# Batch 0's last latent attention moved into the last cross attention of batch 1, its norm in three ticks

## The chip, the cores and the metric

One core of a Trainium2 chip runs the whole program. The metric is the device time of one execution in microseconds, as the median of several; the profile is one execution more, with its own time. All data is float32, so each matmul shows as two instructions in the trace, while a transpose is one.

## The reference

The input x has 2 batches of 512 tokens of 128 values, the context has 2 batches of 77 keys of 64 values. The stages are a latent attention (L0), a cross attention (L1), a decoder of six layers (L2) and a last latent attention (L3). The change touches the last one:

```python
q = emb @ Wq + bq                     # emb: the decoder's output, per batch 512 x 128
k, v = latent @ Wk + bk, latent @ Wv + bv      # latent: the context, 77 x 64
w = softmax((q @ k.T) / sqrt(E), axis=tokens)  # over the 512 tokens, for each of the 77 keys
x = w @ v + emb
out = (x - mean(x)) * rsqrt(var(x) + 1e-6) * gamma + beta
```

Each decoder layer has self attention (16 heads), cross attention over the 77 keys (16 heads) and a feed-forward of 512 hidden units, each behind a layer norm and with a residual.

## The kernel before, in words

The decoder is one flat program for each engine. A planner (class Unit) counts ticks; at each tick it lists what is issued, and every engine walks through the ticks in the same order, skipping what isn't its own. Work is done in chunks of 128 tokens: a score matmul (line 1039), the masked minimum on VectorE (L1495), the exponentials on ScalarE (L1281), the scaling by the reciprocal of the sums on GpSimd (L673), the transposes ("turns", L1051), their evacuation into PT by VectorE (L1513 in the cross attention), and, for a group of four chunks, the "attend" matmuls which add into one PSUM bank, sum (L1081). A tick of the cross attention of batch 1 has a turn every second tick and an attend step in the others. TensorE's order within a tick is: scores, attend steps, early jobs, the turn, jobs. VectorE's order is: reciprocals, the evacuation of the turn of the tick before, jobs of the tick before (of "out", three ticks before), the scaling of the last values, norm steps, masked minima. ScalarE runs the jobs of the tick before, then the last exponential, then the chunk's exponentials, then the eviction of sum (L1313).

Around the change, in the last layer: x1 is tick 488, at which the cross attention of batch 1 starts; it ends at tick 512 ("after"). Batch 0's feed-forward is in it: hidden products (job h, L876) at 496 and 497, the output product (job out, L907) at 498, its add into X (L1409) by VectorE at tick 501. From 513 to 514 the last attend steps are issued. Then follows batch 1's chain: eviction of sum (514), transposes back (job fin, L859, tick 515), the add into X (L1409, tick 516), its norm (statistics L1333, L1337, L1339; the root on GpSimd, L634; scaling L1344; ticks 516 and 517), the turned norm (job xn, L871, tick 519; the copy L1165), the hidden products (521) with their evacuation (L1179), the output product (522) and the add.

The last latent attention of a batch has six steps, whose ticks the tuple LAST_AT gives, counted from x1 + 14 = 502 for batch 0 and from 526 for batch 1: transposes of X (job x3, L703, copied by ScalarE, L1176); the score product for all tokens (job s3, L896) with the minimum on VectorE (L1359); the exponential on ScalarE (L1123); the reciprocal of its sum and the scaling of the values on VectorE (L1365, L1367); the value product (job p3, L729) with its add into X (L1409); the norm z with gamma and beta behind it (function finish, L1522, L1525), after which the output transfer of the batch is issued (L616). Before the change batch 0 has these at ticks 514, 516, 516, 519, 520 and 521. PSUM results of the jobs rotate over three banks (W0 to W2). GpSimd also adds a bias to X after batch 1's norm (L686).

Of the kernel before, what the change touches and what calls it, by code (L numbers as in the profile page):

```python
# [143 lines left out]
AFTER_X0 = (0, 2, 3, 4, 5, 7)  # L144
AFTER_X1 = (2, 3, 4, 4, 5, 7)
LAST_AT = (12, 14, 14, 17, 18, 19)
FEED0 = ((8, 8, 9, 9), 10, (13, 14, 15, 17))
FEED1 = ((9, 9, 9, 9), 10, (18, 18, 20, 21))


class Unit:
# [90 lines left out]
            self.jobs[at + kv] += [("k", j, b, i), ("v", j, b, i)]  # L242
            self.jobs[at + keys] += [("G", j, b, i, 0), ("G", j, b, i, 1)]

    def last_attention(self, b, at, steps):

        turned, scores, exps, scaled, values, norm = steps
        self.jobs[at + turned].append(("x3", self.layers, b))
        self.jobs[at + scores].append(("s3", self.layers, b))
        self.late[at + exps].append(("exp3", b))  # L250
        self.late[at + scaled].append(("scale3", b))
        self.jobs[at + values].append(("p3", self.layers, b))
        assert values < norm
        self.normalise(at + norm, ("z", self.layers, b, 3), (0, 0, 0))

    def last_operands(self, at):
        for i, what in enumerate(("k3", "v3", "g3")):
# [7 lines left out]
    def place(self):  # L265
        for b in range(B):
            self.early[1 + 4 * b].append(("xn", 0, b, 0))
        first = [[(kind, 0, i) for kind in ("ck", "cv")] for i in range(3)] + [[("cG", 0, i, r) for r in range(2)] for i in range(3)]
        for events, dt in zip(first, WEIGHTS0_AT, strict=True):
            self.jobs[1 + dt] += events  # L270
        self.self_operands(0, 0, 1, (0, 2, 4, 6))
        for j in range(self.layers):
            s0, s1, x0, x1 = (self.start[j, k] for k in range(4))
            after = self.end[j, 3]
            for i, dt in enumerate(CV_AT if j > 0 else CV0_AT):
                self.jobs[s0 + dt].append(("cV", j, i // 3, i % 3))
            self.self_operands(j, 1, s0, SELF1_AT)
            self.after_attention(j, 0, 0, s1, AFTER_S0)
            self.after_attention(j, 1, 0, x0, AFTER_S1)
            if j + 1 < self.layers:  # L280
                for (kind, *i), dt in zip(WEIGHTS, WEIGHTS_AT, strict=True):
                    self.jobs[s1 + dt].append((kind, j + 1, *i))
                self.self_operands(j + 1, 0, x1, SELF0_AT)
            self.after_attention(j, 0, 1, x1, AFTER_X0)
            self.feed_forward(j, 0, x1, *FEED0)
            self.after_attention(j, 1, 1, after, AFTER_X1)
            self.feed_forward(j, 1, after, *FEED1)
            if j + 1 == self.layers:
                self.last_operands((s1 + 30, s1 + 31, s1 + 33))
                self.last_attention(0, x1 + FEED0[1] + 4, LAST_AT)  # L290
                self.last_attention(1, after + FEED1[1] + 4, LAST_AT)

    def place_wide(self):
# [1287 lines left out]
```

How the kernel before makes its waits and increments, by code:

```python
        @block.sync  # L470
# [89 lines left out]
            sp.dma_start(norm_b[:], col(a["L2_xattn_norm_b"])).then_inc(sem("norm_in"), 16)  # L560
            load_o(0)
            sp.dma_start(cross_bias[:].bitcast(I32), a["mask_Bx1xS2_if1"].rearrange("b a m -> a b m").broadcast_to([P, B, M]))\
              .then_inc(sem("cross_mask_in"), 16)
            sp.dma_start(b2[:], a["L2_xattn_ff_b2"][0:L].rearrange("(a l) p -> a l p", a=1).broadcast_to([P, L, E]))\
              .then_inc(sem("b2_in"), 16)
            def emptied(unit, event, l):
                sp.wait_ge(sem(unit.ring.free(event)), unit.ring.value(event, l))
            sp.wait_ge(sem("L1_done"), 1)
            load_cross_o(0)
            load_ff(0)
            sp.wait_ge(sem("X_biased"), B)
            load("L3", "Wk", "Wq", "bk", "bq", "Wv")
            load_rows("L3", bv["L3"], "bv")
            load_rows("L3", gam["L3"], "gamma")
            load_rows("L3", bet["L3"], "beta")
            sp.wait_ge(sem("flag"), 1)
            general = sp.value_load(flag[0:1, 0:1], min_val=0, max_val=1)
            with sp.If(general < 1):
                for j in range(L):
# [6 lines left out]
                                emptied(FAST, event, 0)  # L588
                            else:
                                sp.wait_ge(sem(PRE.free(event)), PRE.value(event, 0))
                        load_q(j + 1)
# [114 lines left out]
            def key_operands(s, bank, l=0):  # L706
                pe.wait_ge(*loaded(s, "Wk"))
                if s == "L3":
                    pe.wait_ge(*loaded(s, "Wq"))
```

## Time and profile before

| | us |
|---|---|
| median of 3 runs | 1084.78 |
| lowest, highest | 1083.2, 1084.96 |
| profiled execution | 1083.69 |
| its span, first to last instruction | 1081.9 |
| TensorE busy | 1025.6 (95%) |
| ScalarE busy | 804.2 (74%) |
| VectorE busy | 719.9 (67%) |
| GpSimd busy | 392.1 (36%) |

The span begins at the first instruction; all positions below are microseconds from there. The decoder ends with batch 1's last steps, so the last 35 us of the span are the place of interest. [...]

### The profile page before, as it was taken

The numbers are of one execution on the slowest core, as the hardware profiler recorded it, in microseconds if no ns is written. First come the engines' busy times: TensorE is split into PE (matmuls) and PEld (weight loads), VectorE is DVE, ScalarE is ACT, GpSimd is POOL, SyncE is SP. The second block draws the span as 40 slices with busy tenths as digits, with TensorE's granted clock in tenths as the row PEclk, the third lists the DMA queues.
The fourth block names the chain that finished last, engine by engine and source line by source line (L and its number), as shares of the span: only waits on it lengthen the run. The fifth ranks groups of instructions, "written<-read, shape, count | busy, mean of one in ns | idle before, by whom it ended". The sixth has DMA issues, their size and how long they took to land.

```text
span 1081.9 us, 20513 instructions
## 1 busy us (share of the span) xinstructions
PE 1025.6 (95%) x5146; PEld 605.4 (56%) x5146; DVE 719.9 (67%) x4492; ACT 804.2 (74%) x3518; POOL 392.1 (36%) x404
## 2 busy tenths in 40 slices
PE   7899999999999999999999999999999999999984
PEld 5555455665555655555655555655555556555553
DVE  4666778556778566677765678656678855678744
ACT  3586988666998576898676798666798866699831
POOL 4133443233443233443333344223344322344420
PEclk9899999999999999999999999999999999999997
DMA  8402000003100002200002200001300000000000
GB/s 231 139 6 66 1 21 1 1 1 86 59 21 1 1 1 79 67 1 21 1 1 79 67 1 21 2 1 56 90 1 21 1 2 1 21 1 2 1 1 23
DMA packets 31802, 32.39 MB, mean 30 GB/s; under 512 B 3982, under 2 KB 27710, under 8 KB 30910
## 3 DMA queue, kind: packets, MB, share of 16 engines
q1 hardware_dynamic: 28542, 28.38, 9.4%
q10 hardware_dynamic: 3136, 2.62, 0.8%
q8 instruction: 46, 0.75, 0.3%
q14 instruction: 78, 0.64, 0.2%
HBM read 30.47 MB, written 0.52 MB: 29 GB/s over the span
## 4 chain that ended last, share of the span: by engine, by line
PE 85%; DVE 6%; ACT 5%; issue 3%; POOL 1%; DMA 0%; DVEq 0%; SPq 0%; ACTq 0%
PE S L1039 23%; PE T L1051 11%; PE sum L1081 10%; PE W L852 8%; PE sum L1065 7%; PE W L876 4%; PE W L907 4%; PE W L794 3%; PE W L831 2%; PE W L814 2%; PE W L809 2%; PE W L871 2%; DVE Pb L1495 2%; DVE XN L1344 2%; ACT Pb L1281 2%
## 5 line engine op out<-in xcount | busy, mean ns | idle before, releaser
L1281 ACT ACTIVATE Pb<-Pb,mn 128x128 f32<-128x128 f32 (+1 forms) x1536 | 561.0, 371 | 39.1 <-DVE mn L1495 38.6
L673 POOL TENSOR_TENSOR Pb<-Pb,rsum 128x512 f32<-128x512 f32 (+2 forms) x336 | 324.8, 971 | 606.2 <-DVE rsum L1503 606.1
L1281 ACT ACTIVATION_READ_ACCUMULATOR Pb<-Pb,mn 128x1 f32 x1536 | 295.0, 192 | 0.0
L1495 DVE CUSTOM_DVE_ANT_0 Pb<-S,late_bias 128x128 f32<-128x128 f32 x768 | 175.9, 286 | 124.3 <-PE S L1039 124.0
L1051 PEld LDWEIGHTS T<-ident,Pb 128*128 128x128 f32 (+2 forms) x1296 | 164.0, 146 | 155.4 <-issue 124.1
L1039 PE MATMUL S<-GV,XT 128*128 128x512 f32 x384 | 199.1, 605 | 1.9 <-DVE mn L1495 0.8
L1051 PE MATMUL T<-ident,Pb 128*128 128x128 f32 (+2 forms) x1296 | 197.1, 273 | 1.4 <-POOL Pb L673 1.4
L1513 DVE COPY PT<-T 128x512 f32<-128x512 f32 (+1 forms) x240 | 155.9, 650 | 59.8 <-PE T L1051 59.6
L1495 DVE CUSTOM_DVE_ANT_0 Pb<-S,cross_bias 128x77 f32<-128x77 f32 x768 | 131.8, 232 | 64.8 <-PE S L1039 62.6
L1081 PE MATMUL sum<-PT,Vc 128*128 128x512 f32 (+2 forms) x264 | 135.1, 601 | 0.2 <-DVE PT L1513 0.2
L1039 PE MATMUL S<-Gc,XT 128*128 128x462 f32 (+1 forms) x288 | 125.7, 521 | 3.5 <-DVE mn L1495 2.1
L1495 DVE DVE_READ_ACCUMULATOR2_ANT mn<- 128x1 f32 x1536 | 126.3, 82 | 0.0
L1039 PEld LDWEIGHTS S<-GV,XT 128*128 128x128 f32 x384 | 61.8, 190 | 56.2 <-issue 41.2
L852 PE MATMUL W<-PT,GV 128*64 128x512 f32 x384 | 93.0, 605 | 0.0
L1065 PE MATMUL sum<-o_pair,saow 128*128 128x512 f32 x192 | 90.3, 592 | 0.0
L1292 ACT ACTIVATE PT<-T 128x512 f32<-128x512 f32 x96 | 56.4, 587 | 27.1 <-PE T L1051 26.3
L1039 PEld LDWEIGHTS S<-Gc,XT 128*128 128x128 f32 x288 | 45.6, 190 | 34.7 <-issue 22.2
L634 POOL TENSOR_TENSOR rstd<-veps,minus_half 128x4 f32<-128x4 f32 x40 | 40.5, 1012 | 67.0 <-DVE veps L1339 66.0
L1081 PEld LDWEIGHTS sum<-PT,Vc 128*128 128x128 f32 (+2 forms) x264 | 44.9, 190 | 27.8 <-issue 24.4
L1503 DVE RECIPROCAL rsum<-sums 128x4 f32<-128x4 f32 (+1 forms) x336 | 58.4, 174 | 0.9 <-ACT Pb L1281 0.6
L1065 PEld LDWEIGHTS sum<-o_pair,saow 128*128 128x128 f32 x192 | 35.6, 190 | 39.2 <-issue 39.2
L1179 ACT ACTIVATE hT<-W,small 128x512 f32<-128x512 f32 x48 | 32.9, 687 | 22.5 <-PE W L876 22.2
(173 smaller groups left out, 1067.7 us busy)
## 6 DMA issues: line engine op xcount, KB each, us to landing
sakv<-in_L_xattn_sa_kv SPq DMA_DIRECT2D x6, 1024.0 KB, 5.6
caq<-in_L_xattn_ca_q SPq DMA_DIRECT2D x6, 512.0 KB, 7.1
saq<-in_L_xattn_sa_q SPq DMA_DIRECT2D x6, 512.0 KB, 5.7
cakv<-in_L_xattn_ca_kv SPq DMA_DIRECT2D x12, 256.0 KB, 7.9
saow<-in_L_xattn_sa_ow SPq DMA_DIRECT2D x6, 512.0 KB, 4.3
w<-in_L_xattn_ff_w SPq DMA_DIRECT2D x12, 256.0 KB, 3.0
caow<-in_L_xattn_ca_ow SPq DMA_DIRECT2D x30, 96.0 KB, 2.7
GV<-in_mask_BxSxS_ik ACTq DMA_DIRECT2D x1, 1536.0 KB, 11.7
```

The source lines that it names most:

```text
L673: nc.gpsimd.tensor_tensor(rows, rows, r, ALU.mult).then_inc(sem(f"{unit.name}_weights"), 1)
L852: last = nc.tensor.matmul(w[half(h), :], v_own[:, b, p // TB, c:c + D], PT[:, g % 2, p % 2 * 2 + h, :], start=True, stop=True)
L876: last = nc.tensor.matmul(w[:], w1[:, f * P:(f + 1) * P], XT[:, b * T:(b + 1) * T], start=True, stop=True)
L1039: nc.tensor.matmul(S_ps[n % 2][:, 0:group.columns], XT[:, (b * TB + qt) * P:(b * TB + qt + 1) * P], keys, start=True, stop=True).then_inc( ...
L1051: last = nc.tensor.transpose(T_ps[n % 2][0:k1 - k0, t * P:(t + 1) * P], Pb[:, n % SLOTS, k0:k1], ident[:])
L1065: mm = nc.tensor.matmul(sum_ps[:], saow[:, p, :], o_pair[:, p % 2, :], start=(p == 0), stop=(p == NPAIR - 1))
L1081: mm = nc.tensor.matmul(sum_ps[:], vals, PT[0:k, g % 2, blk, :], start=(group.first and blk == 0), stop=(group.last and at_end))
L1281: last = nc.scalar.activation(Pb[:, s, t * w:(t + 1) * w], Pb[:, s, t * w:(t + 1) * w], ACT.Exp, bias=mn[:, s, t:t + 1], scale=-1.0, accum ...
L1292: nc.scalar.activation(PT[:, gr % 2, 0:group.blocks, qt * P:(qt + 1) * P], tiles(T_ps[n % 2][:, 0:group.blocks * P]), ACT.Copy)\
L1495: last = nc.vector.tensor_tensor_reduce(out=Pb[:, s, cols], in0=S_ps[n % 2][:, cols], in1=row_bias, scale=1.0, scalar=3.4e38, op0=ALU.add, ...
L1503: nc.vector.reciprocal(rsum[:, n % SLOTS, 0:k], sums[:, n % SLOTS, 0:k])\
L1513: nc.vector.tensor_copy(PT[:, gr % 2, 0:group.blocks, qt * P:(qt + 1) * P], tiles(T_ps[n % 2][:, 0:group.blocks * P]))\
```

## The change

The steps of batch 0's last latent attention get their own tuple, and the three steps of its norm are put on ticks of their own. Counted from tick 502, they are now at 502 (transposes), 504 (scores), 506 (exponential), 508 (scaled values), 509 (value product), and 511, 512 and 513 (norm: statistics; mean, variance and root; scaling and finish). Batch 1's stay as they are. No instruction is added or removed.

```diff
 LAST_AT = (12, 14, 14, 17, 18, 19)
+LAST0_AT = (0, 2, 4, 6, 7, 9)
...
-    def last_attention(self, b, at, steps):
+    def last_attention(self, b, at, steps, by_step=(0, 0, 0)):
...
         assert values < norm
-        self.normalise(at + norm, ("z", self.layers, b, 3), (0, 0, 0))
+        self.normalise(at + norm, ("z", self.layers, b, 3), by_step)
...
                 self.last_operands((s1 + 30, s1 + 31, s1 + 33))
-                self.last_attention(0, x1 + FEED0[1] + 4, LAST_AT)
+                self.last_attention(0, x1 + FEED0[1] + 4, LAST0_AT, (0, 1, 2))
                 self.last_attention(1, after + FEED1[1] + 4, LAST_AT)
```

## Rows read from the trace of the kernel before

**Rows 1.** The page: busy time of TensorE, and its share in 40 slices.
```profile
PE 1025.6 (95%) x5146; PEld 605.4 (56%) x5146; DVE 719.9 (67%) x4492; ACT 804.2 (74%) x3518; POOL 392.1 (36%) x404
...
PE   7899999999999999999999999999999999999984
```

**Rows 2.** The chain of waits from 1037 us: start, duration, piece.
```profile
1037.48 0.44 PE T L1051 x4
...
1039.11 1.05 PE sum L1081 x2
...
1040.49 0.86 PE sum L1081 x2
...
1042.87 3.57 PE sum L1081 x8
...
1046.46 0.70 ACT oT L1313
...
1047.29 0.64 PE W L859 x4
...
1050.29 0.69 DVE OP L1359
...
1054.14 2.05 PE W L729 x8
1056.19 5.34 PE W L876 x8
```

**Rows 3.** Timeline, 1047 to 1063 us: start, duration, engine, line, idle before.
```profile
1047.96 0.69 DVE L1409 TENSOR_TENSOR X<-W,X 128x512 f32<-128x512 f32 x1 [4.50 <-PE W L859]
...
1050.39 1.02 POOL L634 TENSOR_TENSOR rstd<-veps,minus_half 128x4 f32<-128x4 f32 x1 [8.44 <-DVE veps L1339]
...
1052.64 1.27 POOL L686 TENSOR_TENSOR X<-X,b 128x512 f32<-128x512 f32 x1 [1.23 <-DVE XN L1344]
...
1052.71 1.28 DVE L1367 TENSOR_SCALAR L0vo<-L0vo,orec 77x128 f32<-77x128 f32 x1
...
1053.55 0.78 ACT L1165 ACTIVATE XT<-W,small 128x512 f32<-128x512 f32 x1 [1.72 <-PE W L871]
...
1057.01 0.87 DVE L1333 BATCH_NORM_STATS2 stats<-X 128x6 f32<-128x128 f32 x4
...
1062.06 0.69 DVE L1525 TENSOR_TENSOR X<-X,L0bet 128x512 f32<-128x512 f32 x1
```

**Rows 4.** Timeline of batch 1's last latent attention, 1067 to 1079 us.
```profile
1067.60 0.60 ACT L1176 ACTIVATE XT<-W 128x512 f32<-128x512 f32 x1 [5.37 <-PE W L703]
...
1070.16 0.72 ACT L1123 ACTIVATE OP<-OP,omin 77x512 f32<-77x512 f32 x1 [1.97 <-DVE omin L1359]
...
1071.25 0.28 DVE L1367 TENSOR_SCALAR L0vo<-L0vo,orec 77x128 f32<-77x128 f32 x1
...
1071.68 1.13 PE L729 MATMUL W<-L0vo,OP 77*128 77x128 f32 x8 [2.28 <-DVE L0vo L1367]
...
1073.62 0.87 DVE L1333 BATCH_NORM_STATS2 stats<-X 128x6 f32<-128x128 f32 x4
...
1078.29 0.69 DVE L1525 TENSOR_TENSOR X<-X,L0bet 128x512 f32<-128x512 f32 x1
```

**Rows 5.** Timeline of the last cross attention, 1036 to 1044 us.
```profile
1036.94 0.68 DVE L1409 TENSOR_TENSOR X<-W,X 128x512 f32<-128x512 f32 x1
...
1041.25 0.70 POOL L673 TENSOR_TENSOR Pb<-Pb,rsum 128x308 f32<-128x308 f32 x1 [0.68 <-DVE rsum L1503]
...
1042.90 0.56 DVE L1513 COPY PT<-T 128x384 f32<-128x384 f32 x1 [0.63 <-PE T L1051]
```

**Rows 6.** Windows of TensorE: stretch, its length, PE busy, granted clock, DMA.
```profile
35.95:42.70 6.75, 6.75 (x27) 0.50 0.56 148
1048.90:1052.70 3.80, 0.00 (x0) 1.00 0.00 0
1053.10:1059.80 6.70, 6.07 (x16) 0.50 0.00 1
1060.00:1066.00 6.00, 5.22 (x36) 1.00 0.15 44
```

## The prediction

> **What bounds the kernel now.** I read the page first: TensorE is busy 95% of the span, and in the slices only the last, where PE shows 4, is loose [rows 1]. So work moved earlier goes from a loose stretch into a full one. The chain of waits shows where the border lies. Up to 1046.46 us every long piece is PE, one matmul group behind the other without a gap: this is the last cross attention of batch 1 [rows 2]. From 1046.46 on it passes from engine to engine, one small step each: eviction of the sum, four transposes, the add into X, the norm, again transposes, then batch 1's feed-forward, then batch 1's latent attention [rows 2, 3, 4]. Nothing else has to be done in that tail but batch 0's latent attention, which the change moves. In the tail the reader should look for two things: what of batch 0's work stands on the chain, and what it stands beside.
>
> Of its four parts one is on the chain. The value product of batch 0 (line 729, eight instructions, 2.05 us) runs from 1054.14 to 1056.19, and batch 1's first hidden product, which is behind it in TensorE's order, starts at 1056.19 [rows 2]. What that product needed was ready before: the copy of the turned norm into XT ran 0.78 us from 1053.55, so it ended at 1054.33, and 0.14 us later (the gap between the end of the eviction at 1047.16 and PE's next piece at 1047.29) the hidden product could have begun, at 1054.47 [rows 2, 3]. So 1056.19 - 1054.47 = 1.7 us hang on the moved work. The transposes, the score product and the minimum of batch 0 lie in waits of batch 1's chain: the minimum (0.69 us at 1050.29) ends at 1050.98, while GpSimd's root, on which the norm waits, takes 1.02 us from 1050.39 and ends at 1051.41 [rows 2, 3]. Batch 0's own last norm and its scaling (1057.01 to 1062.75) lie beside batch 1's feed-forward and free nothing when they go [rows 3].
>
> **Part one: what TensorE gets in the full stretch.** Three jobs go in. Transposes of X: four instructions, 0.44 us at the pace of the turns there [rows 2]. The score product with 512 columns: two instructions, 0.86 us, as each attend step of the same width [rows 2]. The value product: eight instructions of 128 columns; alone at full clock 1.13 us [rows 4], at the pace of the turns (0.11 each) 0.88 us [rows 2]. I take 0.95, as PE has other work on both sides of it. Sum 2.25 us. Their cost is the full sum, since PE has no gap there, except where a gap is behind them anyway.
>
> Does the cross attention stall besides? I followed the ticks. The transposes come when four more turns are to follow, at 1037.9, and need the add of batch 0's feed-forward, which ran from 1036.94 to 1037.62 [rows 5]: no wait. ScalarE's copy (0.60 us [rows 4]) is done near 1039.05, the score product starts near 1039.5: no wait. VectorE's minimum (0.69) then ends near 1041.1, and behind it is queued the reciprocal of the last chunk but one, on which GpSimd's scaling (0.70) and then a turn wait. Before, that stood clear; now the scaled chunk is there at about 1042.0, and PE comes to that turn at 1042.45, being 1.3 us later itself: slack 0.4 us. The exponential has nothing behind it on ScalarE but the eviction; from its start at 1070.16 to the end of the scaling at 1071.53 the second batch took 1.4 us [rows 4], so this can be done by 1042.9, VectorE's evacuation and reciprocal between them included. But the scaling's one instruction took 1.28 instead of 0.28 us in the first batch, where GpSimd's 1.27 us add ran beside it from 1052.64 [rows 3, 4]. Now GpSimd's last chunk (0.70 us [rows 5]) is beside it: it ends at 1043.2 at the worst, and PE reaches the value product at 1043.64. The add of that product (0.69) stands ahead of the last evacuation (0.56) on VectorE, which so ends near 1045.8 instead of 1043.46 [rows 5]; the attend step that needs it could begin at 1045.76, and begins at 1045.95. Before it began at 1043.73 (1042.87 plus 0.86) [rows 2]. So the attention ends **2.2 us** later, at 1048.66. The product, transposes and scores also take PSUM banks in their new places; each bank's last reader there (the feed-forward's, done by 1037.62) is done before. Bounds: 1.8 us, if the first gap of 0.2 us (the attend piece of 1.05 instead of 0.86 us at 1039.11 [rows 2]) and part of the product's cost are swallowed; 3.2, if one of the two slacks is used up.
>
> **Part two: what VectorE has in the way.** The three ticks of the norm order it statistics, variance, scaling, finish, all ahead of batch 1's add after the attention. It can't begin before the last evacuation, 1045.8. The second batch's run of the same list took from 1073.62 to 1078.98, that is 5.36 us, with GpSimd's root in it [rows 4]; the first one's from 1057.01 to 1062.75, 5.74 us [rows 3]. So it ends at 1045.9 + 5.36 = 1051.3 (1051.7 by the other). Batch 1's add, which before started at 1047.96, would be ready at 1047.96 + 2.2 = 1050.15. VectorE executes in order, so the add waits behind the norm's last steps until 1051.3: **1.15 us** more. Three ticks spread the norm's waits, but there are no ticks with other VectorE work between them, so they hide nothing. On GpSimd the root moves ahead of batch 1's, near 1047.5, where nothing is queued behind it; the output transfer of batch 0 starts some 11 us earlier on SyncE's queue, with nothing behind it but batch 1's. From below this is 0 (if the norm began 1.2 us earlier), from above 1.55.
>
> From the add on, the chain to the hidden product is as before but without the value product: before 1047.96 to 1054.47, so now 1051.3 + 6.5 = 1057.8. Before it was 1056.19. That is **+1.6 us**: 2.2 + 1.15 - 1.7, 1.65 unrounded.
>
> **Part three: the clock.** [...] So the first hidden products run at half speed now: 5.34 us for eight instructions, where at 0.86 for two they would take 3.44, so 1.9 us are paid already [rows 2]. After the change PE stands idle longer (fin at 1050.1 to the turned norm at 1056.1), and the value product, which was 2.05 us of activity ahead of the hidden products, is gone. The level will be low at 1057.8 too. If the clock comes back 3.7 us after the hidden products begin, as now, nothing changes; if it takes as long as in the first stretch, 6.8 us, three more microseconds run at half pace, which costs 1.5 us. I take **+0.4 us**, nearer the first because the row of this very stretch shows it. Behind it, feed-forward and latent attention of batch 1 are unchanged. Chance of a gain: if the clock didn't fall, -1.9.
>
> [...]
>
> **Sum.** +2.2 + 1.15 - 1.7 + 0.4 = +2.0 us (2.05). The profiled execution took 1083.69 us, 1081.9 of it the span and 1.8 around it; with the change that is 1085.7. The median of the three runs is 1084.78, 1.1 above the profiled one, and they spread by 1.8. Against the median: **1086.8 us**, own spread +1.2 to +3.0.
>
> **Rivals.**
> The slower side: the clock returns late. Condition: hidden products begin after 6 us of idleness, and the clock stays low as long as in the first stretch, through nearly all hidden products. Price: 1.5 instead of 0.4 us, total +3.1 or more; it decides against "no change" where the clock returns over 4.7 us after the hidden products begin (1.65 plus half of one microsecond). For it: the absent activity. Time 1088.0.
>
> A stall in the attention: the minimum, or the exponential and scaling of the values, come late, so that a turn or the value product waits for VectorE. Price up to 1 us in part one, total +3: 1087.8. Against it: both slacks are worked out as positive, 0.4 us.
>
> The norm hides: its steps get done before batch 1's add is ready, as if VectorE's idle 4.5 us there sufficed. Then part two costs 0 to 0.3, total +0.9 to 1.2: 1085.8. Against it: 5.36 us of list in 4.3 us of room.
>
> The clock doesn't fall, or returns at once: the hidden products take 3.44 us, total 1.6 - 1.9 = -0.3: 1084.5. Against it: PE's idle time grows. Only with the norm hidden too does this become a gain, -1.4 us.
>
> That the change does nothing can't be: the order of each engine is written out from the ticks.
>
> **How the numbers follow.** A measurement of this kernel can tell about 0.2%, 2.2 us, from no change, so my sum lies just inside. Chances: forecast 0.55 (0.33 below the bound, 0.22 above), late clock 0.2, stall 0.08, norm hidden 0.1, clock stays 0.07 (0.05 within, 0.02 faster; I round this to 0.03). So faster 0.03, same 0.47, slower 0.50. The range of 8 in 10 goes from +0.1 to +4.2 us: 1084.9 to 1089.0. It leaves out the clock that stays, and a late clock together with a stall.
>
> **What would show it.** In the changed kernel: the last attend group ends 2.2 us later, with the value product (line 729, 1.0 us) inside it at full clock; VectorE's add of batch 1 starts right behind the last instruction of line 1525, not behind PE; the hidden products (line 876) follow the copy of the turned norm within 0.2 us, with no line 729 ahead of them, and start 1.6 us later than now; their duration is 5.3 to 6.5 us. I am wrong if the add follows PE directly, if a turn waits for GpSimd in the attention, or if the hidden products take under 4 us or near 7.

## The result, and the profile of the changed kernel

The changed kernel took 1088.72 us as the median of six executions, beside 1084.07 for the kernel before in the same comparison: 4.65 us more, a ratio of 1.0041 with a 95% interval of 1.003 to 1.0051. Ten more executions later gave 1087.19 beside 1084.45, 2.7 us more by the medians and a ratio of 1.003 (1.0019 to 1.004); one of the ten, 1207.45 us at a mean granted clock of 0.843, fell in a slower state of the chip and is left out of both. It is slower, by 0.3 to 0.4%, and the prediction's 1086.8 lies short of it.

The profiled execution took 1090.15 us with a span of 1088.3. Its chain of waits, from the last score product of the decoder on, has the pieces that answer to [rows 2] (start, duration, piece, with rows left out at each "..."; line numbers are one higher than before):

```profile
1039.06 0.52 PE S L1040 x2
...
1040.02 0.44 PE W L704 x4
...
1041.65 0.86 PE W L897 x2
...
1045.74 0.91 PE W L730 x8
...
1051.83 0.69 DVE X L1523
...
1052.60 0.69 DVE X L1526
...
1055.76 1.13 issue
...
1058.14 1.10 PE W L872 x4
...
1060.19 6.08 PE W L877 x8
...
1067.03 3.85 PE W L908 x32
...
1076.43 2.06 PE W L730 x8
```

All three moved TensorE jobs are now on the chain, and so are gamma and beta of batch 0's norm, lines 1523 and 1526. Four things should be seen. First, the chain from the value product passes through VectorE's whole norm of batch 0. Second, the hidden products (L877) have nothing of batch 0 ahead of them. Third, they take 6.08 us where they took 5.34. Fourth, batch 1's own value product, untouched by the edit, takes 2.06 us where [rows 4] has 1.13.

The same on the timeline of the other engines (start, duration, engine, line, tiles, idle before):

```profile
1042.54 0.69 DVE L1360 CUSTOM_DVE_ANT_0 OP<-W,c_key 77x512 f32<-77x512 f32 x1 [0.30 <-PE W L897]
...
1044.49 0.74 DVE L1368 TENSOR_SCALAR L0vo<-L0vo,orec 77x128 f32<-77x128 f32 x1
...
1047.91 0.87 DVE L1334 BATCH_NORM_STATS2 stats<-X 128x6 f32<-128x128 f32 x4
...
1050.83 0.69 ACT L1314 ACTIVATE oT<-sum,small 128x512 f32<-128x512 f32 x1 [6.74 <-PE sum L1082]
...
1051.66 0.63 PE L860 MATMUL W<-ident,oT 128*128 128x128 f32 x4 [0.87 <-ACT oT L1314]
...
1053.20 0.68 DVE L1410 TENSOR_TENSOR X<-W,X 128x512 f32<-128x512 f32 x1
```

Batch 1's add (the last row) shows no idle time ahead of it, where [rows 3] has 4.50 us of waiting for TensorE. TensorE's transposes for it ended at 1052.29. It waited 0.9 us for VectorE's own queue.

The clock, in windows of TensorE that answer to [rows 6] (stretch, length, busy, granted clock with 1.00 for full speed, DMA share, GB/s), first of this profile, then of a second profile of the same kernel:

```profile
1051.00:1054.70 3.70, 0.63 (x4) 1.00 0.11 33
1054.80:1065.00 10.20, 5.90 (x10) 0.50 0.04 12
1066.00:1075.00 9.00, 5.81 (x39) 1.00 0.00 0
1075.80:1078.60 2.80, 2.05 (x8) 0.50 0.01 6
```

```profile
1055.60:1065.80 10.20, 6.60 (x11) 0.50 0.00 0
```

The stretch at a granted clock of 0.50 is 10.2 us long in both, not 6.8, and a second one covers batch 1's value product. That second one isn't new. The kernel before has it too, from 1073.5 us to the end, and neither [rows 6] nor the prediction has this row (`before`):

```profile
1064.00:1073.40 9.40, 4.96 (x34) 1.00 0.08 23
1073.60:1081.90 8.30, 0.00 (x0) 0.50 0.14 39
```

There batch 1's value product had ended at 1072.8, 0.7 us before the clock fell. In the changed kernel the clock fell at 1075.25 and the product began at 1076.43.

One more thing must be taken out before the two profiles are compared. The last score product starts at 1039.06 and not at 1036.96, though nothing ahead of it differs. Among the profiles below it stands between 1036.5 and 1037.4 us, or between 1038.3 and 1039.7. The later place is taken by all six with early steps, but also by two of the six without (behind_hidden, 1039.66, and behind_hidden_warm_last, 1039.37). The whole difference arises in the first 72 us. From there to 1020 us all twelve profiles take the same time to 0.2 us, while the granted clock of the first 72 us differs, in the profile of before and in that of the changed kernel:

```profile
0.00:72.00 72.00, 58.03 (x335) 0.95 0.50 141
```

```profile
0.00:72.00 72.00, 59.57 (x330) 0.88 0.49 141
```

TensorE's granted clock was 0.50 there for 6.8 us before, and for 13.7 and once more 3.4 us in the changed kernel, in code that the edit doesn't touch. I take it for a draw of the execution, and compare from that score product on. From it to the end of the last VectorE instruction the kernel before took 1078.98 - 1036.96 = 42.0 us, the changed one 45.6 us, in its second profile 45.95: **3.6 to 3.9 us** more.

### The profile page after: what moved, and what is told of

It is laid out like the page before. It is cut to its first block, busy times and chain, and to the rows that moved or that the text cites. A ratio compares the mean times of both kernels' runs of the same rounds, so it can differ in the third digit from the quotient of the medians.

```text
span 1088.3 us, 20513 instructions
## 1 busy us (share of the span) xinstructions
PE 1029.8 (95%) x5146; PEld 609.5 (56%) x5146; DVE 719.0 (66%) x4492; ACT 804.4 (74%) x3518; POOL 391.9 (36%) x404
## 4 chain that ended last, share of the span: by engine, by line
PE 85%; DVE 6%; ACT 4%; issue 3%; POOL 1%; DVEq 0%; DMA 0%; SPq 0%; ACTq 0%
PE S L1040 23%; PE T L1052 11%; PE sum L1082 9%; PE W L853 8%; PE sum L1066 7%; PE W L877 4%; PE W L908 4%; PE W L795 3%; PE W L832 2%; PE W L815 2%; PE W L810 2%; PE W L872 2%; DVE Pb L1496 2%; DVE XN L1345 2%; ACT Pb L1282 2%
## 5 line engine op out<-in xcount | busy, mean ns | idle before, releaser
L1040 PEld LDWEIGHTS S<-Gc,XT 128*128 128x128 f32 x288 | 45.6, 190 | 34.7 <-issue 22.2
L1345 DVE TENSOR_SCALAR XN<-X,mv,rstd 128x128 f32<-128x128 f32 x152 | 47.2, 371 | 4.1 <-issue 4.1
```

What stands on the lines that cost most here:

```text
L1040: nc.tensor.matmul(S_ps[n % 2][:, 0:group.columns], XT[:, (b * TB + qt) * P:(b * TB + qt + 1) * P], keys, start=True, stop=True).then_inc( ...
L1345: last = nc.vector.tensor_scalar(dst[:, t, :], X[:, t, :], mv[:, t, 0:1], rstd[:, t:t + 1], ALU.subtract, ALU.mult)
```

## The experiments

Each was timed in five rounds beside the kernel before. Where only LAST0_AT and its steps are edited, the diff is against the changed kernel; `...` stands for lines left out. This table holds what the profiles gave. The columns are: from the last score product to the eviction of sum; from there to the first hidden product; the four hidden products; batch 1's value product; the length of the stretch at a granted clock of 0.50 around the hidden products; the ratio to the kernel before with its interval.

| kernel | scores to eviction | to hidden | hidden | value, batch 1 | low clock | ratio |
|---|---|---|---|---|---|---|
| before | 9.50 | 9.73 | 5.34 | 1.14 | 6.8 | |
| changed | 11.77 | 9.36 | 6.08 | 2.06 | 10.2 | 1.0041 (1.003 to 1.0051) |
| after_again | 11.77 | 9.35 | 6.43 | 2.06 | 10.2 | 1.003 (1.0019 to 1.004) |
| norm_only | 9.51 | 9.71 | 5.13 | 1.14 | 6.8 | 1.0001 (0.9992 to 1.001) |
| late_norm | 11.77 | 8.29 | 6.40 | 2.06 | 10.2 | 1.0021 (1.0009 to 1.0033) |
| value_at_end | 10.60 | 8.30 | 5.47 | 1.14 | 6.8 | 0.9999 (0.9989 to 1.0009) |
| behind_hidden | 9.51 | 8.25 | 6.01 | 1.14 | 6.8 | 1.0004 (0.9994 to 1.0014) |
| before_warm | 9.50 | 8.81 | 3.45 | 1.14 | none | 0.9983 (0.9974 to 0.9992) |
| after_warm | 11.77 | 8.85 | 3.69 | 1.14 | none | 1.0012 (1.0003 to 1.0021) |
| after_warm_last | 11.76 | 9.37 | 5.78 | 1.17 | 10.2 | 1.0032 (1.002 to 1.0044) |
| behind_hidden_warm | 9.51 | 7.73 | 3.67 | 2.06 | none | 0.9973 (0.9964 to 0.9982) |
| behind_hidden_warm_last | 9.50 | 7.74 | 3.67 | 1.17 | none | 0.9971 (0.996 to 0.9981) |

**The same kernel again** (no edit).

> The changed kernel once more, for a second profile and twelve more times. Both theories: from the start of the last score product of the decoder (L1040, unchanged code before it) to the eviction of sum +2.3 us, from there to the hidden products -0.4 us, as in its first profile, since both are order. Theory 1 (clock draws): the hidden products' duration and that of batch 1's value product (2.06 us in the first profile) come out otherwise this time, 5.1 to 6.9 and 1.1 or 2.06; the median stays at +3.5 to +4.7 us. Rival (the slow value product is tied to the change): it shows 2.06 us again.

Measured: 1087.19 us, +2.7. The two order columns repeat to 0.01 us. The hidden products are again slower than before, and the value product showed 2.06 us again, as the rival expected. The kernels below say whether it belongs to the change.

**The norm's three ticks alone.**

```diff
-LAST0_AT = (0, 2, 4, 6, 7, 9)
+LAST0_AT = (12, 14, 14, 17, 18, 19)
```

> The kernel before, with only the second half of the change: batch 0's norm in three ticks (521, 522, 523), everything else at its old tick. VectorE has nothing in those ticks but hidden evacuations on ScalarE beside it, so all theories expect no change: 0 within 0.5 us, and the same chain. If it is slower by over 1 us, spreading the norm costs something of its own and the account of the loss is wrong.

Measured: 1084.88 beside 1084.45, no change within 0.1%. Spreading the norm costs nothing and brings nothing; the move is the change.

**The norm back behind batch 1's.**

```diff
-LAST0_AT = (0, 2, 4, 6, 7, 9)
+LAST0_AT = (0, 2, 4, 6, 7, 19)
...
-LAST0_AT, (0, 1, 2))
+LAST0_AT, (0, 0, 0))
```

> Batch 0's transposes, scores, exponential, scaled values and value product stay where the change puts them; its norm and finish go back to tick 521, behind batch 1's add and norm. Theory 1 (three costs: PE work in the full stretch, VectorE's norm ahead of batch 1's add, clock): the add of batch 1 (L1410) follows PE's transposes again instead of the last instruction of L1526, so the chain is 0.9 us shorter than in the changed kernel, about +3.7 us against the kernel before. Theory 2 (nearly all of the loss is the clock, in the hidden products and in batch 1's value product): removing the norm leaves the idle stretch of PE as long as 5 us, and the time stays at +4.5 us.

Measured: 1086.51 beside 1084.02, +2.5 us (1.0 to 3.6), under the +3.7 and the +4.5 that the two theories gave, which were counted from the first comparison's 4.65. Batch 1's add waits for TensorE again:

```profile
1052.28 0.69 DVE L1410 TENSOR_TENSOR X<-W,X 128x512 f32<-128x512 f32 x1 [4.50 <-PE W L860]
1053.06 0.87 DVE L1334 BATCH_NORM_STATS2 stats<-X 128x6 f32<-128x128 f32 x4
```

From the eviction (1050.78) to the hidden products it is 8.29 us, against 9.36: the norm in the way cost 1.07 us. Of this 0.9 is the add's wait; the four statistics behind it took 0.87 instead of the 1.08 us that they show in the changed kernel. Theory 1 holds in the trace; the medians alone can't tell a microsecond.

**The value product at the end of the attention.**

```diff
-LAST0_AT = (0, 2, 4, 6, 7, 9)
+LAST0_AT = (0, 2, 4, 6, 12, 19)
...
-LAST0_AT, (0, 1, 2))
+LAST0_AT, (0, 0, 0))
```

> As the changed kernel, but the value product at tick 514, behind the last attend step, where PE waits 0.84 us for ScalarE's eviction and before the transposes back; norm and finish at tick 521. Theory 1: the sum ends 0.95 us earlier than in the changed kernel (+1.3 us against before), the product hides but for 0.1 us, the add of batch 0 (0.69) comes before batch 1's add is ready or delays it by at most 0.6, the norm blocks nothing; the hidden products start 0.3 us earlier to 0.3 us later than in the kernel before. With their slower clock (6.1 instead of 5.3 us) +0.7 us, 1084.7. Rival (loss is the attention's disturbance by the early steps as such): +2.5 us as the kernel with the late norm.

Measured: 1084.39 beside 1084.45. The eviction comes 10.60 us behind the scores, 1.17 sooner than in the changed kernel, and this with the transposes and scores still early. So the value product inside the attention cost its own 0.91 us and the wait of 0.26 us for the evacuation queued behind its add; the other two jobs cost 1.1 us (10.60 - 9.50). The product itself hides in the eviction:

```profile
1049.48 1.05 PE L730 MATMUL W<-L0vo,OP 77*128 77x128 f32 x8
1050.57 1.30 DVE L1410 TENSOR_TENSOR X<-W,X 128x512 f32<-128x512 f32 x2 [3.89 <-PE W L730]
```

VectorE's add of batch 0 and that of batch 1 (together the two instructions of the second row) stand back to back here. The expectation was 1084.7. This is a move of the same steps that costs nothing: what it adds to the attention, 1.1 us, it gets back ahead of the hidden products, 9.73 - 8.30 = 1.4 us.

**Filler in the idle stretch**, in the kernel before and in the changed one (with 22 instead of 14).

```diff
+                    if not unit.wide and event[1:] == (FAST.layers - 1, 1, 2):
+                        for t in range(14):
+                            nc.tensor.matmul(w[:, t % TB * P:(t % TB + 1) * P], ident[:], ident[:], start=True, stop=True)
                     if event in unit.norms:
                         pe.wait_ge(sem(f"{unit.name}_norm"), ...)
```

> The kernel before with 14 such matmuls of the identity ahead of the wait for batch 1's last turned norm, in PE's idle stretch from 1048.8 to 1052.7 us. If the clock is the cause of the slow hidden products: they take 3.5 us instead of 5.3, and the value product ahead of them 1.1 instead of 2.05 us, but that waits for VectorE until 1054.1; so it ends at 1055.2 instead of 1056.2. Together -2.8 us, 1081.3 us. Rival (the clock falls all the same, or filler delays the transposes of the norm): 0 to +0.5 us.

> The changed kernel, with 22 matmuls of the identity added on TensorE ahead of its wait for batch 1's last turned norm; their results are overwritten. They keep PE busy through about 5 of its 6 idle us. [...] Against the kernel before: +1.9 - 1.9 = 0, so 1084 us. If batch 1's value product at half clock is regained too, up to 0.9 us less in those runs that had it. Rival: the loss is order alone, and filler does nothing: +4.6 us.

Measured: 1082.32 and 1085.60 beside 1084.02. The filler of the kernel before, and the clock behind it:

```profile
1049.15 3.29 PE L868 MATMUL W<-ident 128*128 128x128 f32 x28
1053.10 0.66 PE L874 MATMUL W<-ident,XN 128*128 128x128 f32 x4 [0.66 <-DVE XN L1347]
1054.62 1.13 PE L729 MATMUL W<-L0vo,OP 77*128 77x128 f32 x8 [0.86 <-DVE L0vo L1370]
```

```profile
1048.90:1052.90 4.00, 3.54 (x29) 1.00 0.00 0
1053.10:1059.80 6.70, 5.22 (x20) 1.00 0.00 1
```

and in the changed kernel:

```profile
1052.47 5.08 PE L869 MATMUL W<-ident 128*128 128x128 f32 x44
1058.41 0.66 PE L875 MATMUL W<-ident,XN 128*128 128x128 f32 x4 [0.86 <-DVE XN L1348]
```

With TensorE busy on nothing useful, the granted clock stays at 1.00, and the hidden products take 3.45 and 3.69 us. That the slow clock around the hidden products follows from idleness is shown by this, in both kernels: none of the four profiles with filler ahead of the turned norm has the low stretch, and each of the eight without it has. In the kernel before it was worth 1.7 us by the medians (2.8 expected, and 2.8 by the traces from the last score product to the end, 42.02 - 39.22), in the changed one 1.2 to 3.1 (of 2.7 to 4.65 us, 1.6 is left, where the expectation had 0, 1.9 us of order less 1.9 us of clock). What is left between the two at a full clock is 3.3 us by the medians, and by the traces 20.62 - 18.31 = 2.3 us to the hidden products and 0.24 in them. That is more than 1.9 from the kernels without filler: at full clock the value product that the change takes away was itself only 1.13 us long, so the move saves less.

**The value product moved the other way**, behind the hidden products.

```diff
-LAST0_AT = (0, 2, 4, 6, 7, 9)
+LAST0_AT = (12, 14, 14, 17, 19, 21)
...
-LAST0_AT, (0, 1, 2))
+LAST0_AT, (0, 1, 4))
```

> The kernel before, with batch 0's value product moved the other way: from ahead of batch 1's hidden products to behind them (tick 521), in the 0.8 us in which PE waits for the last hidden evacuation; its norm's statistics and variance on ticks 523 and 524, beside the output product, its scaling and finish on tick 527, behind batch 1's add. If the account of the chain is right, the hidden products start at the copy of the turned norm plus 0.14 us, 1.7 us earlier, and the value product costs 0.2 us: -1.5 us. Without the value product's 2 us of activity the clock may come back later, which gives up to 1.5 us of it away. Rival: VectorE's finish (2.7 us) lands on batch 1's minimum and eats the gain: 0 to +1 us.

> The value product behind the hidden products as in the kernel of that name, with 14 identity matmuls in PE's idle stretch ahead of the turned norm. There the product's move brought the hidden products 1.5 us nearer by its profile, but they took 0.7 us longer at the lower clock. With the clock kept up they take 3.5 us and the move keeps its gain: 0.8 us less than the kernel before with the filler (1082.3), so 1081.5 us. Rival: the filler's effect and the move's don't add, since the filler alone already shortened the value product to 1.13 us: 1082.3.

Measured without filler: 1084.95 beside 1084.02, no change that can be told (-0.6 to +1.5 us), where -1.5 was expected. The expectation's order came true: 8.25 instead of 9.73 us to the hidden products, and the value product's 0.89 us behind them fill a wait that was 0.76 us long before (1061.53 to 1062.29), so that it costs 0.13 us. But the hidden products ran 6.01 us:

```profile
1057.42 6.01 PE L877 MATMUL W<-XT,w 128*128 128x512 f32 x8 [0.92 <-issue]
```

```profile
1055.40:1062.10 6.70, 5.77 (x10) 0.50 0.00 0
```

They started 1.5 us sooner into the same low stretch and paid 0.67 of it back. By the chain to the output product this profile is still 0.7 us shorter than that of before (24.66 instead of 25.33 us from the scores), which the medians don't confirm. With filler: 1081.53 beside 1084.45, the expected 1081.5, and 0.8 us under the kernel before with filler, though the intervals of those two overlap.

**Filler ahead of batch 1's value product.**

```diff
+                    if unit is FAST and b == 1:
+                        for t in range(8):
+                            nc.tensor.matmul(w[:, t % TB * P:(t % TB + 1) * P], ident[:], ident[:], start=True, stop=True)
                     pe.wait_ge(sem("L3_vo"), b + 1)
```

> The changed kernel with 8 identity matmuls ahead of TensorE's wait for batch 1's scaled values, in its idle 2.3 us before batch 1's value product (2.06 us in both profiles of the changed kernel, 1.14 in the kernel before). If that product is slow because PE idled before it: it takes 1.14 us, -0.9 us against the changed kernel, about +3.0 us against the kernel before by its medians (3.1 and 4.65). The hidden products stay at 6.1 to 6.4 us. Rival: eight matmuls come too late to hold the clock: 2.06 us, no gain.

> The value product behind the hidden products, 14 identity matmuls before the turned norm and 8 before batch 1's value product. [...] With them: 1.14 us in each execution; where it had fallen -0.9 us, elsewhere 0; median 1081.0 us. Rival (the filler stands in the product's way, each is 0.2 us of PE): +0.2 us, 1081.7.

Measured: 1087.83 beside 1084.43 for the changed kernel with it, 1081.23 beside 1084.43 for the other. In both profiles the product ran at full clock:

```profile
1075.27 1.16 PE L730 MATMUL W<-L0vo,OP 77*128 77x128 f32 x8 [0.41 <-DVE L0vo L1371]
```

The clock fell only behind it, at 1080.7 us in the first (42.4 us behind the last score product, later than in any other profile) and at 1075.7 in the second. The medians moved by less than their intervals are wide, so that its 0.9 us come back in the median is not shown. One profile of a kernel without the change, behind_hidden_warm, had the product at 2.06 us and its clock low from 1067.3:

```profile
1067.40:1070.50 3.10, 2.05 (x8) 0.50 0.24 69
```

So a slow value product isn't peculiar to the change, though all three profiles of the kernels with the early value product and without filler had it, and none of the four others without filler. What decides it can be read from where the clock fell. In each of the twelve profiles it fell once more in the tail; in eight of them 0.2 to 4.3 us behind the end of the product, which took 1.13 to 1.17 us, and in the other four 0.8 to 1.2 us ahead of its start, and it took 2.06. In the seven profiles without filler the fall came 35.8 to 36.9 us behind the last score product. The product had ended there after 35.1 to 35.9 us in the four kernels without an early value product, and began after 36.6 to 37.7 in the three with it. So the change meets the fall because its chain is later, and the kernel before missed it by 0.7 us.

The last kernel is the best of all, 3.2 us under the kernel before (0.9971, 0.996 to 0.9981). It has the value product behind the hidden products and filler in both of TensorE's last idle stretches.

## Why the prediction was right, and where it fell short

**What bounds it** held: work from the loose tail went into the stretch where TensorE has no gap, and each of the three jobs is on the chain now, at 0.44, 0.86 and 0.91 us, where 0.44, 0.86 and 0.95 were taken. The one gap there, 0.19 us, was swallowed, and 0.26 us of waiting for the last evacuation came in its place.

**The attention ends 2.2 us later**: 2.27 (11.77 - 9.50), within 0.01 us in each of the five profiles of kernels that keep these ticks. The stall behind the product's add, ahead of the last evacuation, was foreseen too. No turn waited: the reciprocal behind the minimum ran at 1043.16, and the turn followed the attend step at once.

**The norm in VectorE's way, 1.15 us**: the late norm puts it at 1.07.

**The 1.7 us that hung on the value product**: too high. Without product and norm in the way, the hidden products came 1.44 us sooner behind the eviction (9.73 - 8.29), because the turned norm's transposes themselves now run at a granted clock of 0.50, 1.10 instead of 0.80 us. The time without the product was worked out with rows in which they had been at the higher level for about 0.3 us. That is a draw and no effect of the order: norm_only, with the order of before, has 1.09.

So the order cost +1.9 us (21.13 - 19.23) against 1.65 foreseen.

**The clock, +0.4 us**: this is the step that failed, by size. The hidden products lost 0.74 and 1.09 us in the two profiles, since the clock came back 4.8 and 5.5 us after their start instead of 3.7 (1059.86 - 1056.19 before). That is between the value taken and the rival's. An account that fits, read from the profiles and not tested by itself, counts from the transposes of the turned norm, the first work of TensorE after its idle time. From there the clock came back after 7.15 us before (1052.71 to 1059.86) and after 6.9 and 7.6 us in the changed kernel; over the eight profiles with the low stretch it is 5.6 to 7.6. From these transposes to the hidden products it had been 3.5 us, with the value product in between, and is 2.05 now. So about 1.4 us more of the hidden products lie at half pace, an estimated price of 0.7. In behind_hidden, which has no value product there either, the clock came back 4.7 us after the hidden products began.

Beyond this the text said that batch 1's feed-forward and latent attention were unchanged. They were in their order, not in their clock: batch 1's value product lost 0.92 us in both profiles. This term was put at nothing. The trace of before has one more low stretch than the two of [rows 6]: it begins at 1073.5 us, 0.7 us behind that product, and a chain 2 us later runs into it. Order and clock together give 1.9 + 0.74 + 0.92 = 3.6 us, and 3.9 in the second, which are the differences of the two chains. The medians, 2.7 and 4.65 us more, lie around them.

**The rivals.** The late clock (1088.0 us, 0.2) is what came by its own mark, a return over 4.7 us after the hidden products begin. But its price of 1.5 us wasn't reached, and its time lies so near the measured one because of a loss that no rival had, that of batch 1's value product. That is luck. The stall in the attention, the hidden norm and the clock that stays are excluded by the traces. The mechanism was right, the range held, and the weight between "within 0.2%" and "slower" was too even. Both low stretches of the rows were 6.8 us long, so that one of 10.2 us was nowhere to be read; but the 3.7 us were taken because they were of the same place, though the place was to change in how long TensorE idles ahead of the turned norm, 3.87 us before and 5.86 in the changed kernel.

**The beginning of the low stretch**, counted from the last score product, varied between 15.1 and 16.4 us in four profiles of kernels in which TensorE has the same work up to there (after, after_again, late_norm and after_warm_last: 1054.77, 1055.58, 1054.30 and 1053.39, from 1039.06, 1039.16, 1039.01 and 1038.29).

**What stays open.** The low stretch is 6.8 us in four profiles and 10.2 in four, and the long ones are all of kernels with the value product inside the attention. In these TensorE idled for 2.7 to 4.0 us more at the low level before the turned norm's transposes, in the short ones for at most 1.2. This is read from the profiles; no experiment varied that idle time alone. Nor is it settled how often batch 1's value product is slow, which a profile shows once and a median doesn't show, nor whether the later place of the last score product has anything to do with the early steps.

## What to carry to other kernels

Work that stands in an idle tail isn't free to move: first ask, for each part, whether it is on the chain where it is, and whether there is any gap where it goes. Here one of four parts was on the chain, and the three TensorE jobs, 2.21 us long, cost 2.27 us in the full stretch; only gaps that are waits for another engine (the eviction of sum, with 8.30 us from there to the hidden products beside 8.29 in late_norm; the last evacuation of the hidden layer, 0.13 us) took the value product cheaply. And where the matrix engine idles for microseconds in a tail, look at its clock before its order: filler that does nothing was worth more here (1.7 us) than any order tried without it. And a part that is itself unchanged can still pay when its chain gets later, as batch 1's value product did with 0.92 us: look at what the clock does just behind it.

## What was not expected of the hardware

Matmuls of a constant, 3.29 us of them in a stretch of 3.9 us, kept the granted clock at 1.00, and took 1.9 us off the hidden products behind it (5.34 to 3.45). The gain from moving the value product alone, -1.5 us by order, was nearly half paid back to the clock: the hidden products took 6.01 instead of 5.34 us. At the low clock, to start sooner bought less here than it seemed to. And the clock fell once more in the tail of every one of the twelve profiles; whether batch 1's value product took 1.13 or 2.06 us hung on which of the two came first, by as little as 0.2 us (after_warm: product to 1075.0, clock down at 1075.2).
